# Triangular inverse regrouped: from four groups of four tiles (three heads per lane) to two groups of eight tiles (six heads per lane)

## The reference, cut to what matters

```
kk = jnp.einsum('bhid,bhjd->bhij', ki, ki)
T = eye + jnp.where(strict, bi[..., :, None] * kk, 0.0)
rhs = bi[..., None] * (vi - jnp.einsum('bhcd,bhde->bhce', ki, S))
U = jax.scipy.linalg.solve_triangular(T, rhs, lower=True)
```

## Time and profile before

| | us |
|---|---|
| median of 3 runs | 551.8 |
| lowest, highest | 551.0, 553.49 |
| the profiled execution, its own time | 550.21 |
| its span in the profile | 548.4 |

### The profile page before, as it was taken

How to read it: one execution, slowest core, us unless ns; L and a number is a source line. 1 busy time by engine, 2 the same in 40 slices (tenths; PEclk the granted TensorE clock), 3 DMA queues, 4 the chain that set the end, 5 groups by cost and what they waited for, 6 DMA issues and landing times. The chain is left out here.

```text
span 548.4 us, 20441 instructions
## 1 busy us (share of the span) xinstructions
PE 374.8 (68%) x8195; PEld 307.2 (56%) x8195; DVE 335.7 (61%) x753; ACT 195.3 (36%) x436; POOL 192.9 (35%) x302
## 2 busy tenths in 40 slices
PE   0588548664126877699983541289999999999810
PEld 0355335443114766577772431179999999999700
DVE  3647577787743356367776669236666666666517
ACT  3456345333022435377675430132222222222200
POOL 1431111110035122346555320335556656554310
PEclk9979677766556567599997555579999999999975
DMA  5013325225269214567871210111221212231054
GB/s 187 0 47 132 83 75 138 92 86 131 71 148 289 85 47 152 132 219 223 247 209 64 62 60 0 27 46 52 57 55 59 60 58 61 59 57 40 32 196 170
DMA packets 47363, 54.99 MB, mean 100 GB/s; under 512 B 21766, under 2 KB 41766, under 8 KB 47176
## 3 DMA queue, kind: packets, MB, share of 16 engines
q1 hardware_dynamic: 39402, 29.42, 17.8%
q0 software_dynamic: 7616, 23.21, 15.0%
q10 hardware_dynamic: 288, 1.57, 0.7%
HBM read 35.47 MB, written 18.71 MB: 99 GB/s over the span
## 5 line engine op out<-in xcount | busy, mean ns | idle before, releaser
L1439 PE MATMUL ps<-xs,w_up 128*128 128x256 f16 x552 | 78.8, 275 | 0.3 <-issue 0.3
L1555 POOL DMA_INDIRECT d_y<-yo,give x46 | 49.6, 1079 | 66.3 <-DVE yo L1526 59.3
L1542 POOL DMA_INDIRECT row<-d_x,take x46 | 46.1, 1002 | 42.3 <-POOLq L1190 28.5
L1439 PEld LDWEIGHTS ps<-xs,w_up 128*128 x552 | 54.1, 99 | 7.7 <-issue 0.5
L775 POOL TENSOR_SCALAR kx<-kvt,cst 128x192 f32<-128x192 f32 x32 | 29.4, 935 | 69.7 <-PE ps L1074 32.3
L1519 DVE TENSOR_TENSOR hl<-hw,hh 128x512 f16<-128x512 f32 x69 | 49.5, 718 | 2.4
L1483 ACT ACTIVATE xb<-xs 64x256 f16<-64x256 f16 x23 | 9.6, 417 | 114.2 <-DVE xs L1507 114.2
L1526 DVE COPY yo<-ps 128x384 f32<-128x384 f32 x23 | 12.8, 557 | 56.4 <-PE ps L1458 56.4
L1458 PE MATMUL ps<-pjh,hh 128*128 x276 | 45.5, 247 | 0.8 <-DVE hl L1519 0.7
L1458 PE MATMUL ps<-pjh,hl 128*128 x276 | 45.3, 246 | 0.0
L1458 PE MATMUL ps<-pjl,hh 128*128 x276 | 45.3, 246 | 0.0
(11 more groups left out here) (221 smaller groups left out, 933.1 us busy)
## 6 DMA issues: line engine op xcount, KB each, us to landing
pjs<-wproj POOLq DMA_DIRECT2D x8, 576.0 KB, 7.1
d_kv<-kvw SPq DMA_DIRECT2D x8, 384.0 KB, 2.5
d_pt<-ptw SPq DMA_DIRECT2D x16, 192.0 KB, 2.4
kvt<-d_kv SPq DMA_DIRECT2D x16, 192.0 KB, 3.3
pt<-d_pt SPq DMA_DIRECT2D x16, 192.0 KB, 3.1
x_sb<-wfc POOLq DMA_DIRECT2D x8, 384.0 KB, 5.1
fcs<-wfc POOLq DMA_DIRECT2D x8, 384.0 KB, 5.5
d_q<-qw SPq DMA_DIRECT2D x8, 192.0 KB, 2.7
```

The lines of the kernel that those rows point to most:

```text
L1439: last = nc.tensor.matmul(ps[:, NP * u + m // 2, (m % 2) * WIDE:(m % 2 + 1) * WIDE], w[k][:, m * 128:(m + 1) * 128], x, start=(k == 0), st ...
L1542: nc.gpsimd.indirect_dma_start(row[s % RB][:, half, :], None, d_x.rearrange("p t c -> (p t) c"), bass.IndirectOffsetOnAxis(ap=take[:, at:a ...
L1555: nc.gpsimd.indirect_dma_start(d_y, bass.IndirectOffsetOnAxis(ap=give[:, at:at + 1], axis=0), yo[s % YB][:, half, :], None).then_inc(s_ysc ...
```

## The change

- `QT, HS` go from 4, 4 to 2, 2. A group is eight tiles: 8 x 8 = 64 lanes per set of heads (`LP`), two sets, six heads per lane (`LH` = 6). Each elimination instruction has twice the elements, and there are 60 instead of 120 of them. The runs of `load_lanes` and `store_lanes` are 384 bytes, in 2 DMAs instead of 4.
- Group 0 (batches 0 to 3) is loaded after batch 3 and done in batches 4, 5 and 6; SyncE waits for it after its step of batch 6 and stores it. Group 1 is loaded after batch 7, at the end of the mix stage, and done in the scan: six columns before the loop and two in each iteration, until c = 4.
- The inverse of tile 8 (before: of tile 12) waits for the store of the last group.
- `xh` and `xl` move to tensors of the routing stage, and with them their eight GpSimd settings, from the scan's stage to the start of routing; TensorE waits there for all eight (`one_rows`). `unit_lanes` runs twice, not four times, over tensors of twice the size.

```diff
-QT, HS = 4, 4
-INVERSE = ((0, 0, 3, 5, 7), (7, 9, 11, 13, 15))
+QT, HS = 2, 2
+LP = 128 // HS
+INVERSE = {4: (0, 0, 1, 3, 4), 5: (4, 5, 6, 8, 9), 6: (9, 10, 11, 13, 15)}
...
             for g in range(HS):
-                eng.dma_start(lanes[32 * g:32 * g + 32, :, :, :].rearrange("p i h j -> p i (h j)"),
-                              d_n[4 * q:4 * q + 4, :, :].rearrange("t (c i) w -> (t c) i w", i=CH)
+                eng.dma_start(lanes[LP * g:LP * g + LP, :, :, :].rearrange("p i h j -> p i (h j)"),
+                              d_n[8 * q:8 * q + 8, :, :].rearrange("t (c i) w -> (t c) i w", i=CH)
                               [:, :, g * LH * CH:(g + 1) * LH * CH]).then_inc(done, 16)
...
-                        if b % 2:
-                            q = b // 2
+                        if b == 3:
                             for j in range(2):
                                 sp.wait_ge(st_n[j], ONE + 16 * (b + 1))
-                            load_lanes(sp, lane_n[q], q, ln_ld[q] if q < QT - 1 else last_ld)
-                            if q:
-                                sp.wait_ge(s_inv, ONE + 2 * (CH - 1) * q)
-                                store_lanes(sp, lane_m[q - 1], q - 1, st_m[q - 1])
+                            load_lanes(sp, lane_n, 0, ln_ld)
+                        if b == 6:
+                            sp.wait_ge(s_inv, ONE + 2 * (CH - 1))
+                            store_lanes(sp, lane_m, 0, st_m)
+                    for j in range(2):
+                        sp.wait_ge(st_n[j], ONE + 16 * B)
+                    load_lanes(sp, last_n, 1, last_ld)
...
-                        if c == 4 * (QT - 1):
+                        if c == NT // 2:
                             sp.wait_ge(last_st, 16 * HS)
...
-                    for u in range(4):
-                        chain(nc.gpsimd.memset(xh[u][HC:HC + 1, :, :], 1.0))
-                        chain(nc.gpsimd.memset(xl[u][HC:HC + 1, :, :], 0.0))
...
-                    for m in range(5):
-                        eliminate(dve, last_n, last_m, m, last_inv, 0)
+                    for m in range(6):
+                        eliminate(dve, nc.vector, last_n, last_m, m, last_inv, 0)
...
-                        for m in range(min(5 + 2 * c, CH - 1), min(7 + 2 * c, CH - 1)):
-                            eliminate(dve, last_n, last_m, m, last_inv, 0)
+                        for m in range(min(6 + 2 * c, CH - 1), min(8 + 2 * c, CH - 1)):
+                            eliminate(dve, nc.vector, last_n, last_m, m, last_inv, 0)
...
             def _(pool):
+                for u in range(4):
+                    nc.gpsimd.memset(xh[u][HC:HC + 1, :, :], 1.0).then_inc(one_rows, 1)
+                    nc.gpsimd.memset(xl[u][HC:HC + 1, :, :], 0.0).then_inc(one_rows, 1)
+                pool.wait_ge(one_rows, ONE + 8)
...
             def _(pe):
+                pe.wait_ge(one_rows, ONE + 8)
```

More of the change, by code:

```diff
@@ L140, in eliminate @@
             eng.wait_ge(done, first + 2 * m + 1)
-            nc.vector.tensor_tensor(below, below, pr, ALU.subtract).then_inc(done, 1)
+            math.tensor_tensor(below, below, pr, ALU.subtract).then_inc(done, 1)
         held_by[0] = early
@@ L233, in program @@
             s_inv = sem("s_inv")
-            ln_ld = [sem(f"ln_ld{q}") for q in range(QT - 1)]
-            st_m = [sem(f"st_m{q}") for q in range(QT - 1)]
+            ln_ld, st_m = sem("ln_ld"), sem("st_m")
             with nc.Block() as block:
@@ L286, in _ @@
                         sp.wait_ge(st_q[u], ONE + 16 * (B // 2))
-                    for q in range(QT - 1):
-                        sp.wait_ge(st_m[q], ONE + 16 * HS)
-                        sp.wait_ge(st_m[q], ONE + 16)
+                    sp.wait_ge(st_m, ONE + 16 * HS)
                 @block.gpsimd
@@ L655, in program @@
         owner = sb("owner", [1, SL], mybir.dt.int32)
-        xh = [sb(f"xh{u}", [HC + 1, 2, TP], f16) for u in range(4)]
-        xl = [sb(f"xl{u}", [HC + 1, 2, TP], f16) for u in range(4)]
         count16 = sb("count16", [128, TP], f16)
@@ L1170, in program @@
         x16 = [sbr(f"x16{u}", [128, 2 * C], f16) for u in range(4)]
+        xh = [sbr(f"xh{u}", [HC + 1, 2, TP], f16) for u in range(4)]
+        xl = [sbr(f"xl{u}", [HC + 1, 2, TP], f16) for u in range(4)]
         xw = [sbr(f"xw{u}", [128, C]) for u in range(4)]
```

30 lines of the change are left out of this document (15 added, 15 removed).

## The result

| | kernel before | changed kernel |
|---|---|---|
| median of 4 runs, us | 551.43 | 535.07 |
| lowest, highest | 551.0, 553.49 | 533.75, 539.29 |
| the profiled execution, its own time | 550.21 | 533.75 |
| its span in the profile | 548.4 | 532.1 |

The ratio of the times is 0.971 (95% interval 0.965 to 0.977). The forecast was 530.0 with a range of 524 to 537. So direction and range hold, but the gain is 16.3 us and not 21.8. The whole study that follows is about these 5.5 us.

The account below looks back on a forecast made before the run. It took VectorE's elimination to bound the mix stage. Mix stage -18.7, hand-over -5.0, scan +0.9 and routing +1.0 sum to -21.8 us: 528.4 against the profiled 550.2, median 530.0, range 524 to 537.

Parts of the forecast that it names:

- The price of an elimination: VectorE's elimination instructions: 154 ns fixed plus 1.764 ns per element; a group 11.8 us before, 19.0 after.
- -16.5: Mix stage: three small elimination groups go and one large one comes, 19.0 - 35.5 us, all on the path.
- The elimination lies wholly on the path: Mix stage, step with columns 7 to 14: VectorE busy grows by 5.96 us, time by 6.38, so no elimination is hidden.
- The wait for lanes: Mix stage: VectorE's waits of 5.0 us become one in batch 4 of 2.3 us (1.5 to 3.5), net -2.7.
- those for squares: Mix stage: larger columns fill the wait from batch 5 to 6, -1.6 us; batches 2 and 3 lose time, +1.0.
- The hand-over: From mix stage to scan: lane store and landing leave the path, 9.8 us become 4.8, -5.0 (-5.5 to -2.5).
- delays there only stores nobody waits for: Hand-over: group 0's store stands behind batch 6 and was taken to hold up nothing on the path.
- 1.7: Hand-over: landing time of the last d_n store, part of the 4.8 us (1.7 + 2.4 + 0.7).
- transfers go by bytes: Rival: batch 4's wait, hand-over and tile 6's queue each 2.7 us worse from doubled bytes; 538 us, chance 0.07.
- +0.5: Scan before the loop: larger columns delay the first uo; TensorE's stall end may not depend on it (0 to 1.2 us).
- The queue of tile 6: Scan, c = 4: fewer columns and store DMAs ahead of tile 6's loads, -0.8 us (-1.2 to +2.6).
- The rivals on TensorE's clock: Half clock in batches 2 and 3, 532.5 us, chance 0.12; one scan iteration either way, 526 or 534, chance 0.12.

Follow-up runs that it names:

- second traces: A second profiled execution of each kernel, both unchanged; the last nw came at 145.8 us before and 131.2 us after.
- first pair: The first traces of the kernel before and the changed kernel, both unchanged; the profiled executions took 550.21 and 533.75 us.
- second pair: Second traces of the kernel before and the changed kernel, both unchanged; the last nw came at 145.8 and 131.2 us.
- the reorder alone: Kernel before, with the last group's store issued behind kvt and qt of tile 7, not ahead of tile 6's loads: median 538.9 us, ratio 0.978.

## Why the prediction was right, and where it was short

**The price of an elimination: right.** Sum of durations of group 0 19.2 us (forecast 19.0), three small groups 35.2 (35.5); in the second traces 19.7 and 36.4.

**The mix stage, -16.6 instead of -18.7 (-14.9 by the means of four executions each).** The step that failed is the sum of durations taken as time on the path, in three ways.
- Of the -16.5, 16.1 is left by durations, but VectorE's busy time in the stretch falls by 13.9. The last three instructions of the kernel before lay behind the last `nw` (146.61 to 147.45, beside the store at 146.44 in the earlier trace rows), 0.8 us that cost nothing there. Another 0.6 is durations that overlap with the next instruction's, more often with 90 instructions than with 30. Both can be read from the trace of before. And two `nw` instructions in a row of the changed kernel took 0.51 and 0.87 us instead of 0.36 each.
- "The elimination lies wholly on the path" holds for the step that I checked it on, and for the difference of the two kernels (14.8 by time, 13.9 by busy time). As a statement on the stage it is false: 6 to 7 us are hidden in either kernel. I was lucky that it cancels.
- The wait for lanes is 3.19, within the range but above the 2.3 taken: -1.8 instead of -2.7. This term is loose on both sides: with the same load it was 2.2 to 3.6 us in five executions, and the 5.0 that it replaces was 2.5 in the second trace. The other waits came as forecast: those for squares -0.2 (forecast -1.6 + 1.0), the last scores' 0.93 (1.1). Small gaps gave 1.7 us more than I had counted.

**The hand-over, -3.8 instead of -5.0, and the first mtc, +2.1 instead of +0.3.** The steps that failed are "delays there only stores nobody waits for" and "1.7". The store of group 0 is issued 5 us ahead of the last d_n store, which goes out 0.66 late and lands after 2.95 us instead of 1.68. The load's issue was overestimated (1.28, not 2.4), and what it saved was given back: gts went out 1.15 us after it (0.7), and the next load took 2.53 to issue. I had priced the transfers by the time that their issue takes. Their bytes go on long after the issue (packets of the store issued from 125.39 to 126.67 run until about 131; it lands after 5.3 us, where the small ones took 2.7), and what is sent behind them pays. The load batch by batch shows it from one side (a quarter of the bytes and runs, and 2.1 us are back), the store from ScalarE's queue from the other.

**The rival "transfers go by bytes": true of the store, partly of the load, and it was put too low.** The reading that spoke for the runs as the limit failed: in the store a run of twice the length occupies a DMA engine twice as long (33 ns against 16.5), in the load the longer runs give 30%. Each of its three places came out worse than the forecast, as it said, by 0.9 us, by 3.0 (1.2 and 1.8), and by 1.5 (a gap of 7.78, up by 0.7 where it should have fallen by 0.8), not by 2.7 each. That is 5.4 us together, as much as the whole shortfall (the other errors cancel).

**The scan, +2.9 from the first mtc to the first xw, instead of +0.6.** Before the loop: six columns took 9.0 us instead of 4.0 (forecast 7.0; the last two instructions took 1.32 and 1.68 us), and it cost nothing, since TensorE's stall ended at about its own time: the doubt behind "+0.5" was right, and 0 would have been. c = 1 to 3 cost 1.4, 0.5 and 0.5 in the first pair (forecast 0.9, 0 and 0), but +3.3, -1.7 and -0.2 in the second, so only their sum, 1.4 to 2.4, means something. The step behind them gained 1.1 in both pairs. The queue of tile 6 cost 0.9 (1.2 in the second pair) instead of -0.8, and tile 7's step 0.8 more (0.6). Later steps moved by half a microsecond each way.

**Routing, -0.6 to 0 instead of +1.0.** The first round is late by 1.8 us (forecast 1.5), and the later rounds make it good; in the kernel before the same edit left +0.3 to +1.1.

**The rivals on TensorE's clock came in part.** In the first trace batches 2 and 3, at a granted clock of 0.70 and 0.84, took 11.3 and 10.6 us, under the 12 that was set as the mark. In the trace of the kernel with the queue of tile 6 reordered, whose mix stage is the same, batch 2 took 12.66 us at 0.70, over the mark, and its last `nw` is the latest of the four:

```profile
58.91:71.57 12.66, 11.54 (x246) 7.84 (x252) 7.34 (x17) 7.44 (x16) 2.60 (x3) 0.70 0.26 93
```

That is a part of the shortfall of the means. In the scan the clock came back as before: 1.00 from 233 to 239 us, with 6.0 us for an iteration.

## What to carry to other kernels

A DMA costs those behind it: when transfers are made fewer and larger, look at the issue times and landings of what follows them in the profile, whichever queue it is in, and at how long their packets keep the DMA engines busy, and split the large one so that only what is new comes last. When work is said to be "on the path", leave it out once and read the floor: durations overlap, and the last instructions may lie behind the mark. And a queue that holds loads behind a wait which only a later load needs is worth a look before any tuning of the work in front of it: here the reorder alone gave 12 us by the medians.

## What the runs showed of the hardware

- Two DMAs of 384 KB are issued in 1.28 us, as fast as two of 96 KB (1.20), but one or two of the small DMAs issued within some 2 us behind them take 1.5 to 2.5 us each instead of 0.3 to 0.6 (the first behind the load, `gts`, took 0.31).
- The same store from ScalarE's queue leaves the landing of SyncE's store as late (3.80 us) as from SyncE's own (2.95), or later.
- A lane load takes 5.3 us from issue to use with 384 KB in 2048 runs (four DMAs), 7.0 with 768 KB in 2048 runs (two), 7.9 with 768 KB in 4096 runs (four).
- In the store of lanes the DMA engines move 145 GB/s with 192-byte runs at a busy share of 0.80 and 171 with 384-byte runs at 0.93; in the load 146 and 192 GB/s.
- Stepped access on VectorE costs 1.76 ns per element with a step of 192 bytes (45 and 189 elements in 233 and 487 ns) and 1.73 with 384 (90 and 384 in 312 and 821 ns).
- TensorE stalled in the scan's first iteration until 14.6 and 14.7 us after the first `mtc` in the first traces of both kernels (14.3 to 15.6 in all), whether it had come there 4.4 or 0.9 us before.
